# A fused attention and experts kernel: key tiles taken in pairs with four probability buffers, and the routing of a token tile spread over two heads

## The reference, cut to what matters

```python
q = q / jnp.maximum(jnp.linalg.norm(q, axis=2, keepdims=True), 1e-12)
AB = jnp.einsum('hnd,hmd->hnm', q, q)
AA = jnp.sum(q * q, axis=-1, keepdims=True)
sim = -(AA - 2.0 * AB + jnp.swapaxes(AA, -1, -2)) * HD ** (-0.5)
attn = jax.nn.softmax(sim, axis=-1)
out = jnp.einsum('hnm,hmd->hnd', attn, jnp.swapaxes(v, 0, 1))
```

## Time and profile before

| | us |
|---|---|
| median of three runs | 754.61 |
| profiled execution | 752.73 |
| its span | 751.0 |
| TensorE busy | 657.5 (88%) |
| VectorE busy | 435.3 (58%) |
| ScalarE busy | 386.0 (51%) |
| GpSimd busy | 345.8 (46%) |

### The profile page before, as it was taken

How to read it: one execution, slowest core, us unless ns; L and a number is a source line. 1 busy time by engine, 2 the same in 40 slices (tenths; PEclk the granted TensorE clock), 3 DMA queues, 4 the chain that set the end, 5 groups by cost and what they waited for, 6 DMA issues and landing times.

```text
span 751.0 us, 17613 instructions
## 1 busy us (share of the span) xinstructions
PE 657.5 (88%) x5070; PEld 434.1 (58%) x5071; DVE 435.3 (58%) x1478; ACT 386.0 (51%) x721; POOL 345.8 (46%) x401
## 2 busy tenths in 40 slices
PE   4888899888875999999999999549999999999980
PEld 4776786578642222222222222338999999999970
DVE  0346757775674277777777764436655666566640
ACT  0323338342322899999999998014444444444430
POOL 3111333223231135555555544416777776777771
PEclk9999999999995999999999999569999999999995
DMA  8999999200013990000000000169888988888934
GB/s 333 397 343 339 322 328 340 80 1 1 22 52 118 382 311 32 30 30 30 30 30 30 32 32 31 41 202 295 228 230 230 233 229 229 229 233 229 228 58 74
DMA packets 46063, 124.74 MB, mean 166 GB/s; under 512 B 5243, under 2 KB 31292, under 8 KB 44748
## 3 DMA queue, kind: packets, MB, share of 16 engines
q1 hardware_dynamic: 32780, 108.92, 45.0%
q0 software_dynamic: 11696, 14.19, 9.4%
q10 hardware_dynamic: 1552, 1.18, 0.5%
HBM read 105.53 MB, written 58.42 MB: 218 GB/s over the span
## 4 chain that ended last, share of the span: by engine, by line
PE 71%; DVE 10%; POOL 4%; ACT 4%; DMA 4%; issue 3%; SPq 1%; ACTq 0%; DVEq 0%; POOLq 0%
PE ps L839 14%; PE ps L976 11%; PE ps L826 9%; PE ps L993 9%; PE ps L981 7%; PE ps L680 3%; ACT mid L1080 2%; POOL rstd L467 2%; DMA out<-mid 2%; DVE stat L1165 2%; DVE mid L1173 2%; PE ps L756 1%; PE ps L766 1%; PE ps L653 1%; ACT big L1042 1%
## 5 line engine op out<-in xcount | busy, mean ns | idle before, releaser
L1080 ACT ACTIVATE mid<-ps 128x1536 f32<-128x1536 f32 x144 | 200.3, 1457 | 30.0 <-PE ps L826 30.0
L839 PE MATMUL ps<-mid 128*32 128x384 f32 x1152 | 123.9, 502 | 1.3
L1507 DVE TENSOR_SCALAR mid<-ps,big 128x128 f32<-128x128 f32 x189 | 54.7, 345 | 94.2 <-PE ps L981 56.1
L976 PE MATMUL ps<-mid,big 128*128 128x128 f32 x756 | 96.1, 277 | 0.3 <-ACT mid L1106 0.3
L590 POOL TENSOR_TENSOR mid<-mid 128x384 f32<-128x384 f32 x63 | 62.9, 998 | 70.5 <-DVE mid L1516 47.8
L826 PE MATMUL ps<-mid 52*128 52x512 f16 x432 | 88.3, 390 | 5.5 <-ACT mid L1080 4.9
L976 PEld LDWEIGHTS ps<-mid,big 128*128 128x128 f32 x756 | 90.7, 194 | 0.6 <-ACT mid L1106 0.6
L993 PE MATMUL ps<-big,mid 128*128 x378 | 78.0, 343 | 1.6 <-POOL mid L590 1.5
L1113 ACT ACTIVATE mid<-mid 128x384 f32<-128x384 f32 x63 | 33.0, 523 | 73.3 <-DVE mid L1507 73.3
L541 POOL DMA_INDIRECT expert_in<-big,slot_u x48 | 48.0, 1000 | 46.4 <-DVE slot_u L1398 35.5
L993 PEld LDWEIGHTS ps<-big,mid 128*128 128x128 f32 x378 | 59.7, 189 | 9.3 <-issue 2.1
(11 more groups left out here) (224 smaller groups left out, 1103.3 us busy)
## 6 DMA issues: line engine op xcount, KB each, us to landing
big<-w_cat SPq DMA_DIRECT2D x63, 576.0 KB, 3.9
expert_in<-expert_in SPq DMA_DIRECT2D x16, 1774.5 KB, 46.2
big<-expert_in SPq DMA_DIRECT2D x63, 136.5 KB, 3.5
big<-patches SPq DMA_DIRECT2D x3, 2048.0 KB, 21.2
w_cat<-w_a SPq DMA_DIRECT2D x1, 6144.0 KB, 32.8
big<-w SPq DMA_DIRECT2D x1, 4608.0 KB, 14.7
w_cat<-w_b SPq DMA_DIRECT2D x2, 1536.0 KB, 30.0
big<-patches SPq DMA_DIRECT2D x4, 512.0 KB, 7.6
```

What stands on the lines that cost most here:

```text
L839: last = nc.tensor.matmul(oacc[32 * g:32 * g + 32, 0:QW], vhead[par][:, kb, :], probs[kb % 3][:, g * QW:(g + 1) * QW], start=(kb == 0), st ...
L976: nc.tensor.matmul(banks[half][:, c * P:(c + 1) * P], w1_t[q][:, half * FF + c * P:half * FF + (c + 1) * P], xtT[r][:, 0:P], start=(c == 0 ...
L1080: nc.scalar.activation(probs[kb % 3], SETS[kb % 2], ACT.Exp, scale=0.5).then_inc(probs_ready, 1)
L1507: last = nc.vector.tensor_scalar(glu[r][:, c * P:(c + 1) * P], bank(1 + r)[:, c * P:(c + 1) * P], b1_cols[:, bass.ds(ex * 6 + c, 1)], 7.0, ...
```

## The change

TensorE takes the key tiles in pairs: the scores of kb + 2 and kb + 3, then the weighted sums of kb and kb + 1, with a bank-7 job between the two scores or behind the two sums. A fourth probability buffer is added, and `sums_copy` stands behind the second exponential of a head. The routing of a token tile is spread over two heads: in head n, tile n - 1 gets its `output`, `route`, `route2` and `norm_rows`, and tile n - 2 its `t_transpose`, `logits`, `choose`, `weights`, `weigh`, `ranks`, `place` and `scatter`. For that `t_row`, `slot_u` and the semaphore of the scattered rows exist twice. The six jobs of bank 7 now come in the order `t_transpose`, `logits`, `stacks` 0, `ranks`, `out_transpose`, `stacks` 1. VectorE's and GpSimd's orders follow, and the last head and the end of attention are written anew. The loops cover heads 2 to 9. Of functions that are replaced whole, only the new lines are shown.

```diff
-        t_row = carve(RW)
+        t_row = [carve(RW) for _ in range(2)]
+        probs4 = carve(QS)
         mid = sb("mid", [P, 8448 + NH * STKW])
-        probs = [mid[:, i * QS:(i + 1) * QS] for i in range(3)]
+        probs = [mid[:, i * QS:(i + 1) * QS] for i in range(3)] + [probs4]
...
-        slot_u = sb("slot_u", [P, TOPK], u32)
+        slot_u = [sb(f"slot_u{i}", [P, TOPK], u32) for i in range(2)]
...
+        def head_base(n):
+            return 6 * n - 5 if not isinstance(n, int) or n >= 2 else 2 + 2 * n
...
-            sp.wait_ge(rows_out, 16 * (TOPK * NT + 1))
+            for k in range(2):
+                sp.wait_ge(rows_out[k], 16 * (TOPK * NT // 2 + 1))
...
+            def base_add(r):
+                hr = h_res[:, bass.ds(r, 1), :].rearrange("p a c -> p (a c)")
                 nc.gpsimd.tensor_tensor(hr, hr, ln[:], ALU.add).then_inc(base_ready, 1)
+            def weights(r):
                 held_wait(pool, gd_ready, r + 1)
                 nc.gpsimd.tensor_tensor(wexp[:], euler[:], gd[:], ALU.pow).then_inc(wexp_ready, 1)
+            def scatter(r, par):
                 held_wait(pool, slots_ready, r + 1)
                 for k in range(TOPK):
                     nc.gpsimd.indirect_dma_start(
+                        xs[:, :], bass.IndirectOffsetOnAxis(ap=slot_u[par][:, k:k + 1], axis=0),
+                        t_row[par][:], None).then_inc(rows_out[par], 16)
+            def pool_head(n, par, old=True, prep2=True):
+                pool.wait_ge(oacc_ready, n)
+                head_v(n + 1, 1 - par)
+                if old:
+                    weights(n - 2)
+                if prep2:
                     norm_root(n + 2)
+                route(n - 1)
+                route2(n - 1)
+                base_add(n - 1)
+                if old:
+                    scatter(n - 2, par)
...
+            pool_head(NT - 2, 0, prep2=False)
+            pool.wait_ge(tr_taken, head_base(NT - 1))
             nc.gpsimd.iota(edges, pattern=[[P, NT]], base=0, channel_multiplier=0,
                            allow_small_or_imprecise_dtypes=True).then_inc(plan_consts, 1)
+            route(NT - 2)
+            weights(NT - 3)
+            route2(NT - 2)
+            base_add(NT - 2)
+            scatter(NT - 3, 1)
+            weights(NT - 2)
+            route(NT - 1)
+            route2(NT - 1)
+            scatter(NT - 2, 0)
+            weights(NT - 1)
+            base_add(NT - 1)
...
-                                            probs[kb % 3][:, g * QW:(g + 1) * QW], start=(kb == 0),
+                                            probs[kb % 4][:, g * QW:(g + 1) * QW], start=(kb == 0),
...
+            def pe_head(n, par, old=True, last=False):
+                base = head_base(n)
+                first = isinstance(n, int) and n == 0
+                def ahead(kb):
+                    if kb < KEYB:
+                        scores(par, kb, n * KEYB + (kb - 1))
                     elif not last:
+                        scores(1 - par, kb - KEYB, n * KEYB + (kb - 1))
+                for kb in range(0, KEYB, 2):
+                    if kb + 2 == KEYB and not last:
+                        pe.wait_ge(tr_taken, head_base(n + 1))
+                    ahead(kb + 2)
                     if first:
+                        if kb == 4:
                             pe.wait_ge(b1_ready, 1)
                             stacks(0, n + 1, base)
                         if kb == 8: stacks(1, n + 1, base + 1)
+                    elif last:
+                        if kb == 0: t_transpose(n - 2, par, base)
+                        if kb == 2: logits(base + 2)
+                        if kb == 8: t_transpose(n - 1, 1 - par, base + 4)
+                        if kb == 10: logits(base + 5)
+                    elif not old:
+                        if kb == 6: out_transpose(n - 1, base + 1)
+                        if kb == 8: stacks(1, n + 1, base + 2)
                     else:
+                        if kb == 0: t_transpose(n - 2, par, base)
+                        if kb == 2: logits(base + 1)
+                        if kb == 6: out_transpose(n - 1, base + 4)
+                        if kb == 8: stacks(1, n + 1, base + 5)
+                    ahead(kb + 3)
+                    weighted(n, par, kb)
+                    weighted(n, par, kb + 1)
+                    if first:
+                        pass
+                    elif last:
+                        if kb == 0: out_transpose(n - 1, base + 1)
+                        if kb == 4: ranks(n - 2, base + 3)
+                    elif not old:
+                        if kb == 2: stacks(0, n + 1, base)
+                    else:
+                        if kb == 2: stacks(0, n + 1, base + 2)
+                        if kb == 4: ranks(n - 2, base + 3)
...
+            pe_head(NT - 1, 1, last=True)
+            base = head_base(NT - 1) + 7
+            out_transpose(NT - 1, base - 1)
+            for t in range(NT - 2):
                 last = nc.tensor.transpose(ps[0:E, t * P:(t + 1) * P], comb_all[:, t, :], ident[:])
             last.then_inc(combT_psum, 1)
+            ranks(NT - 2, base)
...
+            for t in (NT - 2, NT - 1):
+                last = nc.tensor.transpose(ps[0:E, t * P:(t + 1) * P], comb_all[:, t, :], ident[:])
+            last.then_inc(combT_psum, 1)
...
-                    if not isinstance(n, int) or n * KEYB + kb >= 3:
-                        act.wait_ge(probs_used, n * KEYB + kb - 2)
-                    nc.scalar.activation(probs[kb % 3], SETS[kb % 2], ACT.Exp, scale=0.5).then_inc(probs_ready, 1)
+                    if not isinstance(n, int) or n * KEYB + kb >= 4:
+                        act.wait_ge(probs_used, n * KEYB + kb - 3)
+                    nc.scalar.activation(probs[kb % 4], SETS[kb % 2], ACT.Exp, scale=0.5).then_inc(probs_ready, 1)
+                    if kb == 1 and not (isinstance(n, int) and n == 0):
...
+            def dve_head(n, par, half, old=True, prep2=True):
+                base = head_base(n)
+                new = base + (3 if old else 0)
+                if old:
+                    tT_copy(base)
+                    choose(n - 2, base + 1)
+                if prep2:
                     prep_squares(n + 2)
+                stack_copy(0, 1 - par, new - (1 if old else 0))
+                stack_copy(1, 1 - par, new - (1 if old else 0))
+                if old:
+                    weigh(n - 2, par)
+                    place(n - 2, par, base + 3)
+                output(n - 1, base + (4 if old else 1))
+                stack_copy(2, 1 - par, base + (5 if old else 2))
+                norm_stats(n - 1, 1 - par)
+                norm_square(n - 1, 1 - par)
+                norm_rows(n - 1, 1 - par, half)
+                if prep2:
                     prep(n + 2)
+            for g in range(3):
+                stack_copy(g, 1, 2 + (0, 0, 1)[g])
+            prep_squares(2)
+            prep(2)
+            dve_head(1, 1, 0, old=False)
...
+            dve_head(NT - 2, 0, (NT - 3) // 2, prep2=False)
+            base = head_base(NT - 1)
+            tT_copy(base)
+            output(NT - 2, base + 1)
+            choose(NT - 3, base + 2)
+            norm_stats(NT - 2, 0)
+            weigh(NT - 3, 1)
+            norm_square(NT - 2, 0)
+            place(NT - 3, 1, base + 3)
+            norm_rows(NT - 2, 0, (NT - 2) // 2)
+            tT_copy(base + 4)
+            choose(NT - 2, base + 5)
+            weigh(NT - 2, 0)
+            base += 7
+            output(NT - 1, base - 1)
+            place(NT - 2, 0, base)
             norm_stats(NT - 1, 1)
             norm_square(NT - 1, 1)
+            norm_rows(NT - 1, 1, (NT - 1) // 2)
             tT_copy(base + 1)
             choose(NT - 1, base + 2)
+            weigh(NT - 1, 1)
             place(NT - 1, 1, base + 3)
             dve.wait_ge(slots_ready, NT)
...
```

More of the change, by code:

```diff
@@ L457, in _ @@
             step(nc.gpsimd.iota(zero_rows[:, TOKEN:RW].bitcast(u32), pattern=[[0, 1]], base=DUMP, channel_multiplier=1))
-            pool.dma_start(out[DUMP:DUMP + P, :], zero_rows[:, 0:C]).then_inc(rows_out, 16)
+            for k in range(2):
+                pool.dma_start(out[DUMP + k * CB:DUMP + (k + 1) * CB, :],
+                               zero_rows[k * CB:(k + 1) * CB, 0:C]).then_inc(rows_out[k], 16)
             t_norm, before_attention = {}, [True] * NB
@@ L562, in _ @@
             pool.wait_ge(buckets_zero, 16 * E)
-            pool_head(0, None, 0, True, False)
+            head_v(1, 1)
+            norm_root(2)
+            pool_head(1, 1, old=False)
             before = step.n
@@ L909, in _ @@
             nc.tensor.transpose(b7[:, 0:E * 6], b1_rows, ident[0:E * 6, 0:E * 6]).then_inc(b1_psum, 1)
[L910 removed]
+            pe_head(0, 0)
+            pe_head(1, 1, old=False)
             with pe.Fori(0, 4) as i:
                 for p in (0, 1):
[L913 to L920 removed]
+                    pe_head(i * 2 + (2 + p), p)
+            pe_head(NT - 2, 0)
```

(40 more changed lines are left out.)

98 lines of the change are left out of this document (17 added, 81 removed).

## The result

The changed kernel takes **769.37 us** (median of 4 runs, 766.33 to 770.85); the kernel before took 754.85 on the same chip (4 runs, 753.69 to 755.52). The ratio is 1.020, 95% interval 1.018 to 1.022. The forecast was 756.0 with a range of 750 to 763: the direction was right, the size not.

The account below looks back on a forecast made before the run. TensorE was taken to set the pace inside attention, busy 18.35 of 18.92 us a head. Loop +4.4, way back +1.2, heads 0, 1 and 11 -2.2, end -2.0 gave +1.4 us: 756.0 us, range 750 to 763.

Parts of the forecast that it names:

- The loop: Loop heads: waits between TensorE and VectorE close into a 19.41 us period against 18.92, +4.4 us over nine periods.
- The six steps of the prediction: One loop head, logits to next logits: 3.05 + 2.27 + 1.43 + 3.53 + 5.33 + 3.80 = 19.41 us.
- step 5: VectorE's query copy 0.82, norm_stats to norm_rows with GpSimd's two turns 3.69, norm_rows 0.82: 5.33 us.
- step 6: VectorE's prep 3.26, tT_copy 0.48, hand-over to TensorE at logits 0.06: 3.80 us.
- under the whole of `prep`: Rival: GpSimd's root and scatters lengthen VectorE's steps; 0.3 us a head is +2.7, 759 to 765; chance 0.12.
- The way back of the hardware loop: Now on VectorE's critical path four times, 0 to 0.47 us each, taken as 0.3: +1.2 us.
- the rival "the clock": TensorE falls to about 89% busy; 10% of attention at 1.2 GHz would add 10 us: 766; chance 0.01.
- Pairs: Key loop: the second weighted sum in a row adds 0.65 us instead of 0.78, saving 0.13 per pair.
- TensorE's own need: Loop head: with pairs and without the border wait, TensorE alone would need 17.3 us.
- Heads 0, 1 and 11: Heads without the old tile or stack jobs: -0.4, -1.6 and -0.2, sum -2.2 us.
- The end: After attention: statistics of tile 11 earlier, -3.2; scatter of tile 10 ahead of its weights, +1.0 to 1.2; sum -2.0 us.

Follow-up runs that it names:

- e9: Changed kernel with 5 small filler products on TensorE ahead of logits and 3 ahead of out_transpose: 761.1 us, ratio 1.010.
- e6: Changed kernel with the indirect stores of tiles 0 to 7 left out: 764.71 us, ratio 1.015.
- e8: Changed kernel with one more unused 128x192 product on VectorE behind norm_rows: 765.98 us, ratio 1.016.
- e3: Changed kernel with 16 small filler products on TensorE ahead of logits and 8 ahead of out_transpose: 768.57 us, ratio 1.013.
- e11: Kernel before with one long unused sum on VectorE ahead of tT_copy: 778.48 us, ratio 1.032.
- e12: Kernel of e5 with one long unused sum on VectorE ahead of tT_copy: 755.66 us, ratio 1.003.
- e2: Changed kernel with norm_stats moved ahead of the query copy on VectorE: 755.94 us, ratio 0.999.
- e1: Kernel before plus key tiles in pairs, four probability buffers and the later sums copy, without spread routing: 757.3 us, ratio 0.999.
- e5: Changed kernel with VectorE's order weigh, output, norm_stats, place, query copy, and ranks after out_transpose: 738.71 us, ratio 0.981.
- e10: Kernel of e5 with the indirect stores of tiles 0 to 7 left out: 739.13 us, ratio 0.981.
- e4: Changed kernel's spread routing without pairs, with three probability buffers and the earlier sums copy: 771.05 us, ratio 1.018.
- e7: Kernel of e2 with the indirect stores of tiles 0 to 7 left out: 743.52 us, ratio 0.986.

## Why the prediction was wrong

**The loop: right, and closed where it was said.** The six steps of the prediction, in the kernel after, from `logits` at 391.26 to the next at 411.19, with these lines at their ends:

```profile
396.62 0.23 DVE L1441 TENSOR_TENSOR slot_oh<-onehot,wexp 128x64 f32<-128x64 f32 x1
...
398.04 0.55 PE L863 MATMUL ps<-ident,o_acc 128*128 128x128 f32 x3 [0.65 <-DVE slot_e L1430]
...
401.56 0.56 DVE L1265 COPY mid<-ps 128x768 f16<-128x768 f16 x1 [2.07 <-PE ps L668]
...
402.35 0.35 DVE L1386 BATCH_NORM_STATS2 stat<-h_res 128x6 f32 x1
...
406.30 0.63 DVE L1403 SCALAR_TENSOR_TENSOR big<-ln,rms,nscale_sb 128x192 f32<-128x192 f32 x1 [1.14 <-POOL rms L533]
...
407.12 0.16 DVE L1241 TENSOR_SCALAR nrmc<-nrm 128x12 f32<-128x12 f32 x1
...
410.16 0.42 DVE L1254 COPY mid<-mid 128x24 f16<-128x24 f16 x1
410.66 0.29 DVE L1410 COPY tT<-ps 128x128 f32<-128x128 f32 x1
...
411.19 0.40 PE L874 MATMUL ps<-gatea_sb,tT 128*128 128x16 f32 x2 [1.27 <-DVE tT L1411]
```

| step | forecast | measured |
|---|---|---|
| 1 logits to stack 0's copy (394.32) | 3.05 | 3.06 |
| 2 key copies | 2.27 | 2.30 |
| 3 weigh, place's first | 1.43 | 1.42 |
| 4 out_transpose to query copy | 3.53 | 3.52 |
| 5 query copy, norms, rows | 5.33 | 5.56 |
| 6 prep, tT_copy | 3.80 | 4.07 |
| sum | 19.41 | 19.93 |

**Two terms of it were too small**, together 0.5 us a head and 4.2 over the nine (head 2, with no store beside it, is only 0.1 over: 19.51 in `e9`). In step 5 the norms took 3.95 instead of 3.69: the prediction read them from the last token tile, 473.92 to 477.61, which is outside the hardware loop. The last token tile of the kernel after took 3.69 as well (489.77 to 493.46). In step 6 `prep` took 3.54 instead of 3.26: the prediction had the scatters "under the whole of `prep`" among its rivals, but priced it by `norm_rows`, which kept its 0.63; the instruction that suffered was another, the last copy, 0.42 instead of 0.18. Without the stores the head is 19.72 (`e6`). The way back of the hardware loop, put at 0.3 us four times (three heads stand behind it), was of the right size where nothing hides it (0.3 us of idle time in `e6` and `e8`), but here it lay under the held copy: heads 4 and 6 took 19.99 and 19.93, heads 7 and 9 19.90 and 19.88. What is left of it is inside the 4.2. These give +4.2 - 1.2 = +3.0 us: 759 instead of 756, within the range.

**The failed step is the rival "the clock", at a chance of 0.01.** It argued that 89% busy is "far nearer to the first" of two readings, 97% at full clock and 49% at 0.63. Two points don't say where between them the clock falls, and a mean share doesn't say how the idle time lies: TensorE kept 88% and stood 1.2 us at one place. So the sum had the idle time in it once, as a longer head, and its effect on the clock at nothing. The low stretches cost some 1.5 us each in four heads (21.37 to 21.52 against 19.9) and 1.0 in head 2 (20.49 against 19.51 in `e9`), **some 7 us** in all. The size that the rival had worked out, +10 us for a tenth of attention, was about right: 17 us of 220 were at 1.2 GHz. By the sum, 756 + 3.0 + 7 + 1.3 (heads 0, 1 and 11 and the end, below) is 767; the other 2 us of the 769.4 are not settled, and the start of attention alone varied by 6 us between profiles.

That idle time brings the low clock is shown by `e3` and `e9` (less idle time, none or less of it), `e11` and `e12` (idle time put into kernels without low clock). It also explains what `e2` gained. From the first to the last sums copy it took 207.6 us where the kernel after had 220.1: -8.0 from loop heads that are shorter at full clock (1.3 at either end, 0.8 in the seven between), -7.2 from the clock, and +2.7 for its last head, which took 19.4.

**Pairs.** What a pair of sums saves was read rightly. In the chain of `e1`, with its columns as in the earlier trace rows, sixteen instructions, that is two key tiles, take 1.43 us where one takes 0.78:

```profile
358.46 1.43 PE ps L840 x16
```

That is the forecast 0.65 for the second. By the Trainium skill (TensorEngine Tiling (Array Packing), Key Properties) a change of the tiling mode drains TensorE; 0.13 us less for the sum that follows its like agrees with it. TensorE's own need, put at 17.3 us a head, shows with the loop open: 17.6 (`e5`), 0.3 more. And `e1` shows that the routing of the kernel before can't use it.

**Heads 0, 1 and 11, and the end.** By the first exponentials of the heads, head 0 took 23.27 us (23.30 before; forecast 0.4 less; it was 22.8 in `e8`, `e9` and `e10`, whose low stretch lay where the kernel before had it) and head 1 17.43 (18.78 before; forecast 17.3). Head 11, from its first exponential to the last sums copy, took 19.35 instead of 19.07, where 0.2 less was forecast; its 16.68 between sums copies looks shorter than 16.88 only because the first of the two copies moved. The three gave -1.1 instead of -2.2. The end: `route` of tile 11 started 2.2 us after the last sums copy, with no indirect store ahead of it, and the statistics after 3.45 us (forecast 3.7; 6.9 before):

```profile
488.49 0.59 POOL L524 TENSOR_TENSOR h_res<-h_res,o_nrm 128x192 f32<-128x192 f32 x1 [1.84 <-DVE o_nrm L1377]
...
489.77 0.35 DVE L1386 BATCH_NORM_STATS2 stat<-h_res 128x6 f32<-128x192 f32 x1
...
498.64 1.06 POOL L542 TENSOR_TENSOR wexp<-euler,gd 128x4 f32<-128x4 f32 x1
```

The four stores of tile 10 then held the weights of tile 11 until 498.64, as expected. Net -1.8 against a forecast of -2.0.

## What to carry to other kernels

When an order of waits closes into a loop that is longer than the busiest engine's work, price the loop step by step as here, and then price the idle time that it gives TensorE a second time: waits of 1.0 to 1.3 us ahead of one job, in heads where TensorE used to be 97% busy, cost 1.5 us more in about half of the heads, through its clock. Before accepting such a loop, look for the engine that stands idle inside it (VectorE, 2.07 us ahead of the query copy) and move work whose inputs are long there (`norm_stats`, `output`) into that place. Take the durations of hand-overs from inside the loop, not from its written-out end.

## What the runs showed of the hardware

- Behind head 0 a stretch at 1.2 GHz lasted 3.4 us or twice that, TensorE was busy for all of it in the two that are shown, and it began 0.4 to 2.3 us behind a place where TensorE had stood for 0.8 to 1.8 us (0.8 in `e9`, 1.8 in `e1`). Waits of 1.0 to 1.6 us in other heads of the same kernels, and some 1.0 us in every loop head of `e4`, brought none. What tells them apart stays open.
- GpSimd's indirect stores reach into other engines' work, by where these stand. In four kernels with stores (`e2`, `e5`, `e8`, the kernel after) VectorE's small copy of 128x24 f16, where it lay beside the stores, ended 0.02 us before the third store did (but for one head of `e8`), in 0.42 or 0.18 us by when it had started; without stores it took 0.18. The Trainium skill (SBUF — State Buffer, SBUF: two separate sides) has an exclusive lock between VectorE and GpSimd, held for a whole instruction, and which a VectorE instruction takes in a two-port mode, or with two SBUF inputs against a GpSimd operation that reads SBUF. An end pinned to the store's end is what such a lock would give. But just before it, under the same store, the copies of 128x192 f16 kept their 0.20 to 0.22 us and the subtraction with two SBUF inputs (L1253) its 0.20, so the trace agrees for this one copy only, and no row shows in which mode each of them ran.
- With scores or filler queued around `logits`, the stores delayed the logits' arrival at VectorE by 0.9 to 1.1 us (`e2`, `e3`). Without stores the delay was gone (`e7`). It was not there either in the kernel after and in `e9`, where TensorE stood idle ahead of `logits`, nor in `e5`, where it did not and a store ran just the same (0.98 us after `tT_copy` in all three). That the stores are needed for it in the order of `e2` is shown; what holds the logits, and why not in `e5`, is not.
